# Moving the head sums of a channel-attention kernel behind the first tile of its second product, and storing whole images

## The reference, cut to what matters

```
xn   = group_norm(x)                      # 32 groups of 12 channels
w    = xn^T @ qkv_w^T                     # first product, 384 x 384
s    = per head and position: sum over the head's 32 channels of w^2 / |w|^2(channel)
Pi   = softmax over the 12 heads of s * temp
dots = sum over positions of Pi_n * w^2   # Pi_n: Pi divided by its sum over positions
u    = -(w * Pi) / (1 + dots)
y    = x + u @ out_w^T + out_b            # second product, 384 x 384
```

## Time and profile before

| | before |
|---|---|
| median of 3 runs | 877.57 us (877.54 to 877.68) |
| the profiled execution, its own time | 877.32 us |
| its span, from first to last instruction | 875.4 us |
| PE busy | 855.1 us, 98% |
| DVE busy | 746.8 us, 85% |
| ACT busy | 528.0 us, 60% |
| granted TensorE clock, mean | 0.995 |

### The profile page before, as it was taken

One profiled execution on the slowest core, in us unless ns is written; L12 is line 12 of the kernel. 1 busy time (PEld: TensorE's weight loads), 2 busy tenths in 40 slices (PEclk: granted clock), 3 DMA queues, 4 the chain that ended last, 5 costly groups with the idle time before them and its releaser, 6 DMA issues.

```text
span 875.4 us, 14196 instructions
## 1 busy us (share of the span) xinstructions
PE 855.1 (98%) x4298; PEld 682.2 (78%) x4298; DVE 746.8 (85%) x1377; ACT 528.0 (60%) x676; POOL 225.5 (26%) x101
## 2 busy tenths in 40 slices
PE   6799999999999999999999999999999999999996
PEld 6577787777787777787777787777787777787785
DVE  7598888898888898888889888898888889888767
ACT  3575556676555676555676555677555677555631
POOL 1321233321233331233331133331133331133300
PEclk9899999999999999999999999999999999999999
DMA  7316655446655445665445665545664545664424
GB/s 279 113 42 220 225 167 192 149 178 215 224 185 192 144 176 201 224 198 179 155 170 196 224 204 173 164 171 187 224 218 159 176 160 187 222 224 153 132 74 165
DMA packets 54996, 158.47 MB, mean 181 GB/s; under 512 B 21442, under 2 KB 25794, under 8 KB 51010
## 3 DMA queue, kind: packets, MB, share of 16 engines
q1 hardware_dynamic: 46192, 155.48, 51.9%
q10 hardware_dynamic: 8786, 2.77, 1.3%
HBM read 105.70 MB, written 52.53 MB: 181 GB/s over the span
## 4 chain that ended last, share of the span: by engine, by line
PE 93%; DVE 3%; DMA 2%; issue 1%; ACT 1%; SPq 0%; DVEq 0%; ACTq 0%
PE acc L498 87%; PE scores L579 5%; DMA PIB<-pi 1%; DMA bias<-in_L_conv_out_b 1%; DVE WS L769 1%; DVE stats L656 0%; PE acc L481 0%; DVE XL L714 0%; DVE UL L841 0%; DMA pi<-PIT 0%; DVE WV L812 0%; DVE W2L L630 0%; DVE W1L L630 0%; ACT WV L408 0%; DVE XN L706 0%
## 5 line engine op out<-in xcount | busy, mean ns | idle before, releaser
L349 POOL TENSOR_TENSOR XL<-XN,XH 128x1024 fp32r<-128x1024 f32 x93 | 222.5, 2409 | 589.8 <-ACT XH L427 589.8
L399 ACT ACTIVATE WS<-acc 128x1024 f32<-128x1024 f32 x96 | 97.9, 1020 | 227.4 <-PE acc L498 213.2
L498 PE MATMUL acc<-XH,W1H 128*128 128x512 f32 x576 | 179.1, 392 | 3.9 <-ACT XH L427 3.7
L498 PE MATMUL acc<-UH,W2H 128*128 128x512 f32 x576 | 178.1, 390 | 2.6 <-ACT UH L389 2.5
L498 PE MATMUL acc<-XH,W1L 128*128 128x512 f32 x576 | 178.4, 391 | 0.0
L498 PE MATMUL acc<-UH,W2L 128*128 128x512 f32 x576 | 177.8, 390 | 0.0
L849 DVE SCALAR_TENSOR_TENSOR X<-acc,bias,X 128x1024 f32<-128x1024 f32 x95 | 118.8, 1276 | 38.0 <-PE acc L498 38.0
L498 PE MATMUL acc<-UL,W2H 128*128 128x512 f32 x576 | 149.9, 396 | 0.0
L769 DVE CUSTOM_DVE_ANT_0 WS<-PIB,WS 128x1024 f32<-128x1024 f32 x96 | 117.3, 1223 | 36.5 <-DMA PIB<-pi 35.8
L498 PE MATMUL acc<-XL,W1H 128*128 128x512 f32 x576 | 147.2, 391 | 0.2 <-DVE XL L714 0.2
L389 ACT ACTIVATE UH<-WV 128x1024 fp32r<-128x1024 f32 x96 | 98.1, 1054 | 78.3 <-DVE WV L795 61.2
(11 more groups left out here) (84 smaller groups left out, 439.9 us busy)
## 6 DMA issues: line engine op xcount, KB each, us to landing
PIB<-pi SPq DMA_DIRECT2D x96, 528.0 KB, 6.1
out_y<-X SPq DMA_DIRECT2D x95, 512.0 KB, 7.4
X<-in_x SPq DMA_DIRECT2D x31, 1536.0 KB, 6.3
gathered<-stats_rows ACTq DMA_DIRECT2D x30, 72.0 KB, 6.7
pi<-PIT SPq DMA_DIRECT2D x96, 16.5 KB
X<-in_x SPq DMA_DIRECT2D x3, 512.0 KB, 4.6
WV<-in_L_conv_qkv_w SPq DMA_DIRECT2D x1, 576.0 KB, 6.7
WS<-in_L_conv_out_w SPq DMA_DIRECT2D x1, 576.0 KB, 7.6
```

The source lines that it names most:

```text
L349: pool.tensor_tensor(XL[:, t, :], XN[:, t, :], XH[:, t, :].bitcast(F32), ALU.subtract).then_inc(xl_done, 1)
L399: act.activation(square_tile(i, t), acc[:, t, :], ACT.Square, accum_out=sumsq[:, t:t + 1]).then_inc(squared, 1)
L498: last = pe.matmul(out[:, h * BANK:(h + 1) * BANK], w[:, k, m * P:(m + 1) * P], r[:, k, h * BANK:(h + 1) * BANK], start=(n == 0 and k == 0 ...
```

## The change

The head sums move from ahead of term (2, 0) of tile 0 to ahead of term (0, 0) of tile 1, that is, behind the whole of tile 0 of the second product. SP stores an image with one transfer of 1536 KB once all three tiles are finished, in place of three of 512 KB; the last image is still stored in parts. The next load into the slot waits for that one store. The last image's attention steps on DVE count on a semaphore of their own (`tile_step`), and wait for it and for `u_step`; the operations themselves are the same. The DVE order is not changed.

```diff
-LAST_ATTENDED, LAST_WEIGHED = 5, 6
+TILE_STEPS = 5
...
-            def store(j, t):
+            def store(j):
                 if has(j):
-                    sp.wait_ge(y_done, j.counts(T, t + 1))
-                    sp.dma_start(j.of(y_img)[:, t * N:(t + 1) * N], x_tile(j, t)).then_inc(y_stored, 16)
+                    sp.wait_ge(y_done, j.counts(T, T))
+                    sp.dma_start(j.of(y_img), X[:, j.slot, :]).then_inc(y_stored, 16)
...
             def step(i):
-                store(i - 2, 2)
+                store(i - 2)
                 if has(i - 2) and has(i + 2):
-                    sp.wait_ge(y_stored, (i - 2).counts(T * 16, T * 16))
+                    sp.wait_ge(y_stored, (i - 2).counts(16, 16))
                     load(i + 2)
                 spread_pi(i)
-                store(i - 1, 0)
-                store(i - 1, 1)
...
+            last = Image(B - 1, B - 1)
+            for t in range(T - 1):
+                store_part(last, t * N, (t + 1) * N, t + 1)
             for h in range(HALVES):
-                store_half(Image(B - 1, B - 1), T - 1, h)
...
-                second_product(i - 1, 0, {(2, 0): lambda: head_sums(i)})
-
-                second_product(i - 1, 1, {})
+                second_product(i - 1, 0, {})
+                second_product(i - 1, 1, {(0, 0): lambda: head_sums(i)})
                 second_product(i - 1, 2, {})
...
             def attend_last(j, t):
...
-                dve.tensor_reduce(total, PIB[:, t, :, QUAD], AX_X, ALU.add).then_inc(u_step, 1)
-                dve.wait_ge(u_step, base + 2)
+                dve.tensor_reduce(total, PIB[:, t, :, QUAD], AX_X, ALU.add).then_inc(tile_step, 1)
+                dve.wait_ge(tile_step, base + 1)
+                dve.wait_ge(u_step, j.counts(U_STEPS, t + 1))
```

More of the change, by code:

```diff
@@ L201, in conv_attention @@
         u_step = sem("u_step")
+        tile_step = sem("tile_step")
         uh_done = sem("uh_done")
@@ L220, in has, with by_tiles, scale_of, wait_weighed @@
             return not isinstance(j.number, int) or 0 <= j.number < B
[L222 to L226, removed]
+        def by_tiles(j):
+            return has(j) and not has(j + 1)
+        def scale_of(t):
+            return dots[:, 3, t:t + 1]
+        def wait_weighed(eng, j, t):
+            if by_tiles(j):
+                eng.wait_ge(tile_step, TILE_STEPS * (t + 1))
+            else:
+                eng.wait_ge(u_step, j.counts(U_STEPS, ATTENDED + t + 1))
+        def in_blocks(tile):
+            return tile.rearrange("p (b n) -> p b n", n=QUAD)
         def norm_of(j):
@@ L288, in _, with store_part @@
                 load(Image(j, j))
-            def store(j, t):
+            def store(j):
                 if has(j):
-                    sp.wait_ge(y_done, j.counts(T, t + 1))
-                    sp.dma_start(j.of(y_img)[:, t * N:(t + 1) * N], x_tile(j, t)).then_inc(y_stored, 16)
-            def store_half(j, t, h):
-                sp.wait_ge(y_done, j.counts(T, t + h + 1))
-                columns = slice(t * N + h * BANK, t * N + (h + 1) * BANK)
+                    sp.wait_ge(y_done, j.counts(T, T))
+                    sp.dma_start(j.of(y_img), X[:, j.slot, :]).then_inc(y_stored, 16)
+            def store_part(j, begin, end, finished):
+                sp.wait_ge(y_done, j.counts(T, finished))
+                columns = slice(begin, end)
                 sp.dma_start(j.of(y_img)[:, columns], X[:, j.slot, columns]).then_inc(y_stored, 16)
@@ L327, in _ @@
             pipeline(sp, step, 0, B)
+            last = Image(B - 1, B - 1)
+            for t in range(T - 1):
+                store_part(last, t * N, (t + 1) * N, t + 1)
             for h in range(HALVES):
-                store_half(Image(B - 1, B - 1), T - 1, h)
-            sp.wait_ge(y_stored, (B * T + HALVES - 1) * 16)
+                store_part(last, (T - 1) * N + h * BANK, (T - 1) * N + (h + 1) * BANK, T + h)
+            sp.wait_ge(y_stored, (B - 1 + T - 1 + HALVES) * 16)
         @block.gpsimd
@@ L384, in u_hi @@
                     if has(j):
-                        act.wait_ge(u_step, weighed(j, t))
+                        wait_weighed(act, j, t)
                         if j.follows(1):
@@ L758, in softmax_divide @@
                 link(dve.tensor_reduce(PIT[:, :, QUAD], PIT[:, :, 0:QUAD], AX_X, ALU.add), follows=False)
-            def in_blocks(tile):
-                return tile.rearrange("p (b n) -> p b n", n=QUAD)
             def dot(j, t):
@@ L800, in attend_last @@
                 total, dot_t, both, inverse = pi_tot[:, t:t + 1], dots[:, 0, t:t + 1], dots[:, 1, t:t + 1], dots[:, 2, t:t + 1]
-                base = j.counts(U_STEPS, t * LAST_WEIGHED)
+                base = TILE_STEPS * t
                 dot(j, t)
-                dve.tensor_reduce(total, PIB[:, t, :, QUAD], AX_X, ALU.add).then_inc(u_step, 1)
-                dve.wait_ge(u_step, base + 2)
[L805 to L810, removed]
+                dve.tensor_reduce(total, PIB[:, t, :, QUAD], AX_X, ALU.add).then_inc(tile_step, 1)
+                dve.wait_ge(tile_step, base + 1)
+                dve.wait_ge(u_step, j.counts(U_STEPS, t + 1))
+                dve.scalar_tensor_tensor(both, total, SUM_FLOOR, dot_t, ALU.add, ALU.add).then_inc(tile_step, 1)
+                dve.wait_ge(tile_step, base + 2)
+                dve.reciprocal(inverse, both).then_inc(tile_step, 1)
+                dve.wait_ge(tile_step, base + 3)
+                dve.scalar_tensor_tensor(scale_of(t), total, SUM_FLOOR, inverse, ALU.add, ALU.mult).then_inc(tile_step, 1)
+                dve.wait_ge(tile_step, base + 4)
                 dve.wait_ge(w_kept, j.counts(T, t + 1))
-                dve.scalar_tensor_tensor(in_blocks(w_tile(j, t)), in_blocks(w_tile(j, t)), dots[:, 3, t:t + 1],
-                                         PIB[:, t, :, 0:QUAD], ALU.mult, ALU.mult).then_inc(u_step, 1)
+                dve.scalar_tensor_tensor(in_blocks(w_tile(j, t)), in_blocks(w_tile(j, t)), scale_of(t),
+                                         PIB[:, t, :, 0:QUAD], ALU.mult, ALU.mult).then_inc(tile_step, 1)
             def finish_half(j, t, h):
@@ L837, in u_lo @@
                     dve.wait_ge(uh_done, j.counts(T, t + 1))
-                    dve.wait_ge(u_step, weighed(j, t))
+                    wait_weighed(dve, j, t)
                     if j.follows(1):
```

## The result

| | before | after |
|---|---|---|
| median | 877.56 us (6 runs, 877.11 to 878.12) | 906.89 us (6 runs, 905.33 to 908.13) |
| ratio to before | | 1.0332, 95% interval 1.0321 to 1.0344 |
| span of the profiled execution | 875.4 us | 903.5 us |
| its own time | 877.32 us | 905.33 us |
| predicted | | 905.5 us, 898 to 911; span 903.3 |

The account below looks back on a forecast made before the run. PE work, 93% of the span, was taken to bound the kernel. 25.8 + 1.42 + 0.56 + 0.1 = 27.9 us took the span from 875.4 to 903.3 us, the median to 905.5 us, range 898 to 911.

Parts of the forecast that it names:

- The bound and the step: Image loop: PE runs without a recorded wait in steps 2 to 31, so a step is its work, 26.15 us.
- The stop: Tile 0 of the second product: PE reaches term (2, 2) 0.75 us before its UL; 0.92 us per loop step.
- The restart's 0.12 us: Behind PE's wait for UL in tile 0: an extra 0.12 us, none at the lower bound, twice at the upper.
- The sums at the border: Head sums between tiles 0 and 1: still 1.65 us, no change; bounds -0.22 to 0.1 us a step.
- loop, steps 2 to 29: 28 loop steps: PE's wait for UL in tile 0 costs 0.92 us each, 25.8 us in all.
- step 1: Unrolled step 1: UL of tile 2 ends at 57.88, so the block of tile 0 and sums ends 1.42 us later.
- step 30: Unrolled step 30, without register counts: UL ends 4.02 us after tile 0 starts; cost 0.56 us.
- from step 31 to the end: Tail: extra wait of 0.03 us in each of three `attend_last`, 0.1 in all; later PIB nothing, at most 1.36.
- The stores and the softmax: Later softmax and PIB transfers, single store and later load: cost nothing; cover for the load 1.4 to 2.5 us.
- The cover: Rival: UL ready early enough, PE never waits, about 876.9 us (chance 0.03), or 870.3 with cheaper sums (0.03).
- The clock: Rival: PE's wait in each step lowers the clock, 3.4 us a step, about 1007 us; chance 0.01.
- The load: Rival: one store and the load take 10.5 us each, load lands late, 3.8 us a step, about 1012 us; chance 0.03.

Follow-up runs that it names:

- e2: The changed kernel with the head sums put back ahead of term (2, 0) of tile 0, leaving the single store and the semaphore; 877.01 us, ratio 0.9998.
- e4: The changed kernel with DVE making UL of tile 2 right behind that of tile 1, ahead of the group moments; 877.77 us, ratio 1.0005.
- e9: The changed kernel with the head sums ahead of term (2, 2) of tile 0 and ahead of that term's wait for UL; 876.42 us, ratio 0.9990.
- e10: The changed kernel with e9's PE order and e11's DVE order joined; 875.93 us, ratio 0.9985.
- e11: The changed kernel with DVE making UL of tile 2 between the head-sum weights and the group norm; 876.94 us, ratio 0.9997.
- e3: The changed kernel with the head sums at term (2, 2) of tile 0, but behind that term's wait for UL; 902.63 us, ratio 1.0294.
- e5: The changed kernel with UL of tile 2 moved behind the statistics of tile 0 on DVE; 966.58 us (median of four runs), ratio 1.1025.
- e1: The kernel before with only the head sums moved behind tile 0, still three stores per image; 910.67 us, ratio 1.0384.
- e13: e4 with the head sums one tile further, ahead of tile 2 of the second product; 1003.16 us, ratio 1.1430.

## Why the prediction was right

*The bound and the step.* PE had no waits, a step was its work, and this held: every kernel that PE doesn't stop in (e2, e4, e9, e10, e11) has a loop step of 26.15 us, wherever the sums stand. The exceptions are single steps: one of 26.70 us in e4, with 0.45 us of idle time that the profile gives no cause for, one of 26.61 in e11, with a short wait for UL, and step 4 before.

*The stop.* UL was said to be ready at T + 4.38 and not to be movable by slack. It is at T + 4.39, though DVE has 1.01 us of slack ahead of the head-sum weights. The cost was put at 0.92 us a step; it is 27.09 - 26.15 = 0.94. The waits were forecast at 21 to 24 us in some 29 stops of 0.7 to 0.8 us; they are 20.4 us in 30, with 0.66 in each loop step. That is not less lost: the profile counts idle time from the modelled end of the matmul before, the 0.81 us from where the next one was due.

*The restart's 0.12 us.* I bounded it from below by nothing, if the emptying for the sums covered it. e3 shows that this bound is real: where the sums themselves end the wait, a step is 26.97 us (486.14 - 459.17 in its timeline of PE), 0.12 less than with a term in between. In the changed kernel a term stands between, and it is paid.

*The sums at the border.* No change was taken, with -0.22 to +0.1 us as bounds. e4 has them at the border without a stop: the sums start at 423.59, 0.10 us behind the 423.50 that nine terms of 0.453 end at, and tile 1 begins 1.43 us later. The step is 26.15 us. The first pair behind the sums takes 0.56 us here too. So the price is the same at the border, as the rule of the Trainium skill (TensorEngine Tiling (Array Packing), Key Properties) on the drain at a mode switch would have it.

*The sum.* Each part of the 28.1 us by which the span grew, from starts in the two timelines:

| part | predicted | measured |
|---|---|---|
| loop, steps 2 to 29 | 25.8 | 758.55 - 732.50 = 26.05 |
| step 1 | 1.42 | 28.02 - 26.92 = 1.10 |
| step 30 | 0.56 | 26.74 - 26.15 = 0.59 |
| start up to step 1 | 0 | 51.92 - 52.22 = -0.30 |
| from step 31 to the end | 0.1 | 38.27 - 37.61 = 0.66 |
| sum | 27.9 | 28.1 |

For the loop, 732.50 is step 30's start of the earlier trace rows less that of step 2 before, 79.14. Step 1 is cheaper because its UL ends at 57.27, T + 5.35, and not at T + 5.66 as before; DVE came to it 0.3 us sooner against PE, which no edit explains. In the tail the three `attend_last` cost 0.02 us and not 0.1; the 0.66 are PE's matmuls at the lower clock in the last product, the stretch 886.4 to 889.9 of the changed kernel:

```profile
380.00:886.00 506.00, 492.21 (x2481) 387.59 (x2480) 423.21 (x775) 299.57 (x380) 128.89 (x54) 1.00 0.48 175
886.40:889.90 3.50, 3.50 (x10) 2.70 (x9) 3.36 (x8) 1.06 (x1) 0.00 (x0) 0.51 0.00 0
```

At half the rate 3.5 us hold 1.75 us of work; part of that loss stands beside waits for UH. That these parts err in both directions makes the sum look better than its parts: a total within 0.2 us is luck, while the loop, 93% of it, is right by itself. The profiled execution took 905.33 us (905.2 forecast); the median lies 1.4 us above the forecast 905.5, by the spread that stays open.

*The stores and the softmax.* "Cost nothing" was right for the changed kernel (e2). What I didn't see is that the single store is what kept it there: with the sums moved and the old stores, PIB's lateness reaches PE (e1).

*The rivals.* The cover was needed; DVE's slack didn't help. The clock stayed up in the loop, as the row with the 0.69 us stop said. That row ends where the stop does and so couldn't show a fall behind it; the whole step 1 before, 52.22 to 79.14, has 1.00 too. e5 shows how near that rival was: that a stop short against the work around it changes nothing held for 0.8 us, and not for 2.0 us in a step of 28.3. The load wasn't late: the waits hold none for it in the loop.

## What to carry to other kernels

Work that an engine does ahead of a wait is cover for what it waits for. Before moving it, write down when each later wait is reached and when its data is ready, and see whether the producer hangs on slack or, as here, on the waiting engine's own progress; in the second case no slack elsewhere helps, and only the order on the producer (e11) or the place of the wait (e9) does. Cover is counted from the place of the wait instruction, not of the matmul that reads the data.

## What the runs showed of the hardware that I had not expected

A stop of PE can cost more than its length. With a stop of 0.8 us in each step the clock stayed at 1.00 from 380 to 886 us; with 2.0 us (e5) it fell to the lower level behind the stop in 15 of 28 steps, 1.6 us extra each, and in two of e5's six runs the mean clock was 0.848 and 0.558. It need not fall even then: PE was idle for some 2.3 us ahead of the last product both before and after the change, and only after it did the clock go down, 1.5 us later. And a single 1536 KB store landed in 6.2 us (6.0 in e2), where three of 512 KB took 7.4 each among the PIB transfers; in e13, with the sums and the softmax later, it took 7.4 as well.
